# A decoder layer's first stage: new opening for batch 1, block-wise first projection, GpSimd subtractions in four pieces, one name column per slot

## The chip, the cores and the metric

One core of a Trainium2 chip runs the whole kernel as one program. The metric is the device time of one execution in microseconds (us), and the profile is one further execution of the same program. The engines are TensorE (PE; its weight loads are PEld), VectorE (DVE), ScalarE (ACT), GpSimd (POOL) and SyncE (SP, which here only starts DMAs). A line such as L704 is a line of the kernel before.

## The reference, cut to what matters

The input `x` has 8 batches of 512 rows of 512 values. Three residual blocks follow each other; the change touches almost only the first.

```python
x = x + attention(layernorm(x))     # 16 heads of 128, gated, decayed, causal
x = x + cross_attention(layernorm(x), ctx, mask)
x = x + ffn(layernorm(x))           # weights rounded to fp8 after a reordering of columns
# attention, per head: q, k, v = silu(x @ w), scores = (q @ k.T) * decay, out = scores @ v,
#   out = norm_w * out / rms(out), gate = sigmoid(x @ w_gate), y = (gate * out) @ w_out
# ffn: W[:, idx], scaled by the row's largest value, rounded to fp8
```

## The kernel before, in words

**Stages.** `attention` (L171) runs first and takes about three quarters of the time, `finish` (L1057 and on) applies the output projection, the cross attention and the FFN tile by tile. Each has one program for each engine; semaphores written by hand set the order.

**Slots.** The attention stage is a loop of 128 slots (`slots`, L318). Slot n works on head pair p = n // 16, batch b and head j of the pair. In each slot PE does, in this order: the decayed scores of the slot (L788, 12 matmuls), the projections of the next slot's q and k and of this slot's gate (L704, 36 matmuls of 512 columns), whatever extra work the slot has, the product of scores and values (L828, 12) and half of the next values (L713, 24). Every product is done in three passes from a high and a low part of both operands, and DVE makes the low parts: L996 for the scores (`sl`, three instructions, which L828 waits for), L855 for q, k and v, with a cast L853 before it.

**Weights.** Each head pair has four weight blocks (V, QK0, QK1, G) of 128x1024. SP loads them to `raw`, ACT copies the high part (`weights_hi`, L540), POOL subtracts to get the low part (`weights_lo`, L433, one instruction for a block). At the last batch of a head pair (slots 14, 30, 46, and so on, then the slot after) the blocks of the next pair are made; V and QK1 come back to back on POOL.

**x.** Each batch of x has to be normed and turned before it can be used. `stats_of` (DVE, L885, L888) takes mean and variance, `norm` (POOL, L454 to L462) makes the factor and the shift from them, `normed` (ACT, L566) applies them, PE turns (L723, L754 for batch 0) and ACT and DVE split the result (`x_hi` L574, `x_lo` L894). Batches 0 and 1 are prepared in the opening, ahead of slot 0, batches 2 to 7 in the slots 0, 1, 3, 5, 7, 9 (`PREPARED`, L186): SP stores their pieces to DRAM (`store_pieces`, L361) and loads them back (L412) for the batch after next. In each prepared slot PE turns three blocks ahead of L828 and one after.

**Names and rows.** The FFN's reordering indices are counted by `add_name` (DVE, L904): 4 columns of 512 and 11 of 1408, grouped by `SUMMED` (L190) into the slots 11 to 15 as 4, 3, 3, 3 and 2 columns. From slot 18 on, one FFN weight tile is masked (POOL), scaled, rounded (DVE) and turned (PE L746) in every three slots, 26 in all (`FIRST`, `STEP`, L188 and L189).

**Opening.** POOL sets constants and clears `sq_sum` (L498), DVE converts a few of them (L948 to L953), then statistics of batch 0, POOL's `norm(0)`, the norming on ACT, 16 turns on PE, the split, and q and k of slot 0 (L704), the turning of batch 1, and the values of batch 0 in two halves (L713), where the second half waits until DVE has read the first half's bank.

Of the kernel before, what the change touches and what calls it, by code (L numbers as in the profile page):

```python
# [15 lines left out]
P = 128  # L16
# [154 lines left out]
def attention(nc, c, early, at, x, w_src, norm_w, slope, ffn, indices, w_outs, dram):  # L171
# [18 lines left out]
    SUMMED = {NAMED - 5 + i: part for i, part in enumerate(  # L190
        [range(0, KD), range(KD, KD + 3), range(KD + 3, KD + 6), range(KD + 6, KD + 9), range(KD + 9, KD + KF)])}
# [24 lines left out]
    for w in (QK1_W, G_W):  # L216
# [28 lines left out]
    nr, kc = sb("newton", [P, 4, KT]), sb("rstd_consts", [P, 4, KT])  # L245
    rs, nb = sb("rstd", [P, 2, KT]), sb("neg_mean_rstd", [P, 2, KT])
# [18 lines left out]
                for l, start, end in (("hi", at.w_out, at.heads), ("lo", at.shared, at.w_out))]  # L265
# [8 lines left out]
    s_xin = [sem(f"x_in{i}_landed") for i in range(3)]  # L274
    s_raw = [sem(f"raw{i}_landed") for i in range(4)]
    s_nw, s_slope, s_ix = sem("norm_w_landed"), sem("slope_landed"), sem("indices_landed")
    s_wh = [sem(f"w{i}_hi_ready") for i in range(4)]
    s_wl = [sem(f"w{i}_lo_ready") for i in range(4)]
    s_pool, s_kc, s_dist = sem("pool_constants"), sem("rstd_consts_ready"), sem("distance_ready")
# [15 lines left out]
    s_sq, s_acc, s_zero = sem("o_squared"), sem("squares_added"), sem("squares_cleared")  # L295
# [3 lines left out]
    s_mag, s_vs, s_round, s_quant = (sem("rows_magnitude"), sem("rows_scaled"), sem("rows_offset"),  # L299
                                     sem("rows_quantised"))  # L300
# [10 lines left out]
    def x_banks(m):  # L311
        return (*S_BANK, G_BANK if m == 1 else Q_BANK)

    def landed(m):

        return s_xin[X_BUFFER[m]], 16 * X_BUFFER[:m + 1].count(X_BUFFER[m])
# [27 lines left out]
    def sync(sp):  # L344
# [25 lines left out]
        sp.dma_start(slope_b[:, :], slope.to_broadcast([P, NH])).then_inc(s_slope, 16)  # L370
        load_x(0)
# [3 lines left out]
        load_raw(QK1_W, 0)  # L375
        load_x(2)
        load_raw(G_W, 0)
        sp.dma_start(nw[:, :], norm_w).then_inc(s_nw, 16)
        sp.dma_start(uix[:, :], indices[0]).then_inc(s_ix, 16)
        sp.dma_start(dix[:, :], indices[1]).then_inc(s_ix, 16)  # L380
        store_x(0)
        sp.wait_ge(s_turned, KD * 2)
        load_x(3)
        store_x(1)
        for n, v, p, b, j in slots():
            if n % (2 * B) == 0 and p + 1 < NP:
                for w in (V_W, QK0_W, QK1_W, G_W):
                    sp.wait_ge(s_wl[w], p + 1)
                    load_raw(w, p + 1)
            if n == LAST + 1 - 2 * B:  # L390
                for w in range(4):
                    sp.wait_ge(s_wl[w], NP)
# [25 lines left out]
            if n in PREPARED:  # L418
                m = PREPARED[n]
                store_pieces(m)  # L420
                if m != 3 and m + 1 < B:
                    nxt = 4 if m == 2 else m + 1
                    sp.wait_ge(s_turned, KD * m + KD)
                    load_x(nxt)
# [5 lines left out]
    def gpsimd(g):  # L430
        def weights_lo(w, p):
            g.wait_ge(s_wh[w], p + 1)
            g.tensor_tensor(wl[w][:, :], raw[w], wh[w][:, :].bitcast(F32), ALU.subtract).then_inc(s_wl[w], 1)  # L433
# [7 lines left out]
        def norm(m):  # L441
# [3 lines left out]
            if m:  # L445
                g.wait_ge(s_nb, m)
            if m >= 2:
                g.wait_ge(s_nm, KT * (m - 2) + KT)

            def did(k, ins):  # L450
                ins.then_inc(s_nrs, 1)
                g.wait_ge(s_nrs, 8 * m + k + 1)
# [31 lines left out]

        g.memset(c.ident[:, :], 0.0).then_inc(s_pool, 1)
        g.memset(tri[:, :], 1.0).then_inc(s_pool, 1)
        g.iota(dist[:, :].bitcast(I32), [[1, S]], base=0, channel_multiplier=-1).then_inc(s_pool, 1)
        g.wait_ge(s_pool, 3)
        g.affine_select(out=tri[:, :], in_=tri[:, :], compare_op=ALU.is_ge, fill=0.0,
                        base=0, pattern=[[1, S]], channel_multiplier=-1).then_inc(s_pool, 1)  # L490
        g.affine_select(out=c.ident[:, :], in_=c.ident[:, :], compare_op=ALU.not_equal, fill=1.0,
                        base=0, pattern=[[-1, P]], channel_multiplier=1).then_inc(s_pool, 1)
        for k, value in enumerate((LN_EPS, -0.5, 1.5, -1.0)):
            g.memset(kc[:, k, :], value).then_inc(s_kc, 1)
        g.memset(c.ones[:, :], 1.0).then_inc(s_pool, 1)
        g.memset(ones16[:, :], 1.0).then_inc(s_pool, 1)
        g.wait_ge(s_kc, 4)
        g.memset(sq_sum[:, :], 0.0).then_inc(s_zero, 1)  # L498
        norm(0)
        norm(1)  # L500
        weights_lo(V_W, 0)
        norm(2)
        weights_lo(QK1_W, 0)
        weights_lo(G_W, 0)
        for n, v, p, b, j in slots():
# [13 lines left out]
            if n + 1 in PREPARED and PREPARED[n + 1] > 2:  # L519
                norm(PREPARED[n + 1])  # L520
            if n == NAMED - 6:
# [5 lines left out]
            g.wait_ge(s_zero, 1)  # L527
            col_b = slice(b * S, (b + 1) * S)
            if n:
                g.wait_ge(s_acc, n)  # L530
            g.tensor_tensor(sq_sum[:, col_b], sq_sum[:, col_b], sq[:, :], ALU.add).then_inc(s_acc, 1)  # L531
# [5 lines left out]
    def scalar(act):  # L537
# [50 lines left out]
        def sig_values(half):  # L588
# [3 lines left out]
            nc.scalar.activation(sig_v[:, :], V_BANK[:, :], ACT.Sigmoid).then_inc(s_sigv, 1)  # L592

        def scaled(n):
# [4 lines left out]
            nc.scalar.activation(v_mag[:, 0:w], rows[:, 0:w], ACT.Abs, scale=w_s[:, s, 2:3]).then_inc(s_mag, 1)  # L599
# [15 lines left out]
        act.wait_ge(s_slope, 16)  # L615
        act.wait_ge(s_dist, 4)
        decay(0)
        weights_hi(QK0_W, 0)
        normed(0)
        weights_hi(V_W, 0)  # L620
        for k in range(KD):
            x_hi(0, k)
        weights_hi(QK1_W, 0)
# [1045 lines left out]
```

## Time and profile before

| | before |
|---|---|
| median of 3 runs | 2697.77 us (2696.01 to 2700.08) |
| profiled execution, its own time | 2699.37 us |
| span of its profile | 2697.6 us, mean granted clock 0.991 |
| PE busy | 2625.0 us, 97% of the span |
| DVE busy | 2123.9 us, 79% |
| ACT, POOL busy | 1066.4 us, 772.8 us |
| opening, up to the first scores matmul | 43.18 us |

The page gives for each engine its busy time and the costliest groups of instructions. The chain of waits follows the work that ended last back to the start; while it stays on one engine, that engine never waits there. A view of stretches gives the busy time and the granted clock (1.00 is 2.4 GHz, one half of it 1.2 GHz) between two times.

### The profile page before, as it was taken

The numbers are of one execution on the slowest core, as the hardware profiler recorded it, in microseconds if no ns is written. First come the engines' busy times: TensorE is split into PE (matmuls) and PEld (weight loads), VectorE is DVE, ScalarE is ACT, GpSimd is POOL, SyncE is SP. The second block draws the span as 40 slices with busy tenths as digits, with TensorE's granted clock in tenths as the row PEclk, the third lists the DMA queues.
The fourth block names the chain that finished last, engine by engine and source line by source line (L and its number), as shares of the span: only waits on it lengthen the run. The fifth ranks groups of instructions, "written<-read, shape, count | busy, mean of one in ns | idle before, by whom it ended". The sixth has DMA issues, their size and how long they took to land.

```text
span 2697.6 us, 39827 instructions
## 1 busy us (share of the span) xinstructions
PE 2625.0 (97%) x14231; PEld 2173.0 (81%) x14231; DVE 2123.9 (79%) x3806; ACT 1066.4 (40%) x1786; POOL 772.8 (29%) x952
## 2 busy tenths in 40 slices
PE   6999899999999999999999999999999999999995
PEld 6888788888888888888888888888877666666662
DVE  7888977877787778778788867876657888888887
ACT  4433333433343343334344423433324445444553
POOL 3111211221131122112212211211123555555555
PEclk9999999999999999999999999999999999999998
DMA  6553322243233324343334422342265555555532
GB/s 230 180 212 141 128 104 104 102 163 121 102 136 131 122 100 137 105 147 119 126 111 147 157 94 94 118 180 94 94 227 173 148 157 161 151 147 160 162 99 54
DMA packets 182499, 366.67 MB, mean 136 GB/s; under 512 B 79264, under 2 KB 82208, under 8 KB 173600
## 3 DMA queue, kind: packets, MB, share of 16 engines
q1 hardware_dynamic: 116480, 339.74, 36.4%
q10 hardware_dynamic: 63488, 15.74, 3.2%
q0 software_dynamic: 2336, 8.65, 1.0%
q8 instruction: 115, 1.88, 0.3%
q14 instruction: 80, 0.66, 0.1%
HBM read 251.75 MB, written 96.61 MB: 129 GB/s over the span
## 4 chain that ended last, share of the span: by engine, by line
PE 95%; DVE 2%; issue 2%; POOL 0%; DMA 0%; ACT 0%; POOLq 0%; DVEq 0%; SPq 0%; ACTq 0%
PE bank L704 39%; PE bank L713 14%; PE bank L1356 13%; PE bank L828 9%; PE bank L788 9%; PE bank L1397 5%; PE bank L1407 2%; PE bank L1386 1%; PE bank L1377 1%; PE bank L1366 1%; PE bank L723 0%; PE bank L746 0%; DMA finish_xs<-in_pad_mask 0%; DVE finish_rt L1559 0%; DVE finish_u L1457 0%
## 5 line engine op out<-in xcount | busy, mean ns | idle before, releaser
L704 PE MATMUL bank<-attention_xT,attention_w_hi 128*128 128x512 f32 x3072 | 956.5, 392 | 2.7 <-DVE attention_xT L894 2.6
L704 PEld LDWEIGHTS bank<-attention_xT,attention_w_hi 128*128 128x128 f32 x3072 | 568.7, 189 | 114.5 <-issue 3.2
L704 PE MATMUL bank<-attention_xT,attention_w_lo 128*128 128x512 f32 x1536 | 599.6, 390 | 0.0
L531 POOL TENSOR_TENSOR attention_sq_sum<-attention_sq_sum,attention_sq 128x512 f32<-128x512 f32 x128 | 206.6, 1614 | 1228.9 <-ACT attention_sq L676 1228.9
L713 PE MATMUL bank<-attention_w_hi,attention_xT 128*128 128x256 f32 x2048 | 383.6, 288 | 3.7 <-DVE attention_sig_v L851 3.7
L704 PEld LDWEIGHTS bank<-attention_xT,attention_w_lo 128*128 128x128 f32 x1536 | 288.8, 188 | 62.1
L713 PEld LDWEIGHTS bank<-attention_w_hi,attention_xT 128*128 128x128 f32 x2048 | 321.1, 193 | 4.0 <-DVE attention_sig_v L851 4.0
L713 PE MATMUL bank<-attention_w_lo,attention_xT 128*128 128x256 f32 x1024 | 291.1, 284 | 0.0
L1356 PE MATMUL bank<-finish_w_out_hi,finish_og 128*128 128x512 f32 x824 | 284.7, 407 | 0.2
L984 DVE TENSOR_TENSOR attention_sf<-bank,attention_dcy 128x512 f32<-128x512 f32 (+1 forms) x256 | 147.8, 619 | 172.4 <-PE bank L788 172.3
L996 DVE TENSOR_TENSOR attention_sl<-attention_sf,attention_sh 128x384 fp32r<-128x384 f32 (+1 forms) x384 | 242.6, 686 | 0.0
L637 ACT CAST attention_sh<-attention_sf 128x384 fp32r<-128x384 f32 (+1 forms) x384 | 186.0, 548 | 124.2 <-DVE attention_sf L984 123.5
L676 ACT ACTIVATE attention_sq<-bank 128x512 f32<-128x512 f32 x128 | 76.9, 601 | 331.4 <-DVE attention_og L1027 331.4
L1027 DVE SCALAR_TENSOR_TENSOR attention_og<-bank,attention_nw,attention_gate 128x512 f32<-128x512 f32 x128 | 95.8, 748 | 133.8 <-PE bank L828 133.8
L713 PEld LDWEIGHTS bank<-attention_w_lo,attention_xT 128*128 128x128 f32 x1024 | 197.6, 193 | 0.0
L1356 PEld LDWEIGHTS bank<-finish_w_out_hi,finish_og 128*128 128x128 f32 x824 | 154.9, 188 | 39.2 <-issue 2.7
L1204 POOL TENSOR_TENSOR finish_t<-finish_silu,finish_u 128x512 f32<-128x512 f32 (+1 forms) x96 | 133.4, 1391 | 160.0 <-ACT finish_silu L1273 156.7
L828 PE MATMUL bank<-attention_sh,attention_vh 128*128 128x512 f32 (+3 forms) x512 | 162.8, 318 | 14.5 <-issue 14.5
L660 ACT ACTIVATE attention_gate<-bank 128x512 f32<-128x512 f32 x128 | 76.6, 598 | 246.5 <-PE bank L704 246.5
L586 ACT ACTIVATE attention_sig_k<-bank 128x512 f32<-128x512 f32 x128 | 76.6, 599 | 239.5 <-PE bank L704 239.4
L828 PE MATMUL bank<-attention_sh,attention_vl 128*128 128x512 f32 (+3 forms) x512 | 166.7, 326 | 0.0
L828 PE MATMUL bank<-attention_sl,attention_vh 128*128 128x512 f32 (+3 forms) x512 | 166.1, 324 | 0.0
(195 smaller groups left out, 4971.7 us busy)
## 6 DMA issues: line engine op xcount, KB each, us to landing
attention_xT<-normed_turned SPq DMA_DIRECT2D x62, 2048.0 KB, 8.5
gated_heads<-attention_og_out SPq DMA_DIRECT2D x64, 1024.0 KB, 7.3
finish_og<-gated_heads SPq DMA_DIRECT2D x103, 512.0 KB, 3.8
finish_og_last<-gated_heads SPq DMA_DIRECT2D x25, 512.0 KB, 3.8
normed_turned<-attention_shared SPq DMA_DIRECT2D x24, 512.0 KB, 6.6
attention_shared<-in_w_head SPq DMA_DIRECT2D x16, 512.0 KB, 7.1
finish_x<-in_x SPq DMA_DIRECT2D x32, 256.0 KB, 4.0
out<-finish_x SPq DMA_DIRECT2D x32, 256.0 KB, 4.3
```

Source lines behind the costliest of these rows:

```text
L531: g.tensor_tensor(sq_sum[:, col_b], sq_sum[:, col_b], sq[:, :], ALU.add).then_inc(s_acc, 1)
L637: nc.scalar.copy(sh[:, a:e], sf[:, a:e]).then_inc(s_sh, 1)
L704: mm = pe.matmul(dst[:, :], part[a][w][:, k, col:col + P], xT[i][:, b, k, :], start=(k == 0 and s == 0), stop=(k == KD - 1 and s == 2))
L713: mm = pe.matmul(V_BANK[:, t * 2 * P:(t + 1) * 2 * P], xT[i][:, b, k, (2 * j + t) * P:(2 * j + t + 1) * P], part[a][V_W][:, k, :], start=( ...
L788: mm = pe.matmul(dst, (kh, kl)[a][:, t * P:(t + 1) * P], (qh, ql)[e][:, Q0[t]:S], start=(s == 0), stop=(s == 2))
L828: mm = pe.matmul(O_BANK[:, Q0[t]:S], (vh, vl)[a][i][:, t, j * P:(j + 1) * P], (sh, sl)[e][:, OFF[t]:OFF[t + 1]], start=(t == 0 and s == 0) ...
L984: v_.tensor_tensor(sf[:, OFF[k]:OFF[k + 1]], S_BANK[k][:, 0:S - Q0[k]], d[:, 0:S - Q0[k]], ALU.mult).then_inc(s_sf, 1)
L996: v_.tensor_tensor(sl[:, a:e], sf[:, a:e], sh[:, a:e].bitcast(F32), ALU.subtract).then_inc(s_sl, 1)
L1027: v_.scalar_tensor_tensor(out=og[:, :], in0=O_BANK[:, :], scalar=nw[:, 2 * p + j:2 * p + j + 1], in1=gate[:, :], op0=ALU.mult, op1=ALU.mul ...
L1204: g.tensor_tensor(t_[:, a:a + w], sg[k % 2][:, 0:w], u_[k % 2][:, 0:w], ALU.mult).then_inc(s_t, 1)
L1356: mm = pe.matmul(Y_BANK[:, :], og[Q % RING][:, j, a, :], wo[b][:, q * HQ + j, :], start=(q == 0 and j == 0 and s == 0), stop=(q == 3 and j ...
L1397: mm = pe.matmul(dst[:, 0:w], qT[m % 2][:, d, :], wT[:, a // P:(a + w) // P, d, :], start=(d == 0), stop=(d == KD - 1))
```

## The change

- The statistics and the norming of batch 0 go tile by tile: four DMAs for x of batch 0 (the slopes come through ACT's queue), `root_of(0)` on DVE instead of `norm(0)` on POOL, ACT applies it to tiles 0 and 1, DVE to tiles 2 and 3.
- The QK0 block of the first head pair is split in four pieces (ACT high, DVE low), and the first q projection waits for each block of x and weights by itself.
- PE runs 160 matmuls of 128 columns on ones (`keep_warm`) from the start, and 12 more after the turns.
- Batch 1 is prepared in slot 0, all four of its blocks ahead of L828; the others follow in slots 1, 2, 4, 6, 8, 10. The second half of the first values goes to another bank and waits for nothing. `sq_sum` is not cleared; its first use is a copy.
- `weights_lo` is four instructions of 128x256 instead of one of 128x1024.
- Names: one column per slot in slots 12 to 26; the FFN weight tiles start at slot 29 instead of 18.
- SP stores the prepared pieces ahead of its other work of the slot.
- Two waits on ACT's magnitude output are dropped, since a later ACT instruction is waited for anyway. In `finish` the last tile's addition goes from POOL to DVE.

```diff
-    PREPARED = {0: 2, 1: 3, 3: 4, 5: 5, 7: 6, 9: 7}
-    NAMED = 2 * B
+    PREPARED = {0: 1, 1: 2, 2: 3, 4: 4, 6: 5, 8: 6, 10: 7}
+    FOLLOWS = {1: 3, 2: 4, 4: 5, 5: 6, 6: 7}
+    COLUMNS = max(PREPARED) + 1
+    NAMED = COLUMNS + 1 + KD + KF
     FIRST = NAMED + 2
-    SUMMED = {NAMED - 5 + i: part for i, part in enumerate(
+    SUMMED = {COLUMNS + 1 + k: k for k in range(KD + KF)}
...
         def weights_lo(w, p):
-            g.wait_ge(s_wh[w], p + 1)
-            g.tensor_tensor(wl[w][:, :], raw[w], wh[w][:, :].bitcast(F32), ALU.subtract).then_inc(s_wl[w], 1)
+            g.wait_ge(s_wh[w], refreshed(w, p))
+            for k in range(KD):
+                ins = g.tensor_tensor(part[1][w][:, k, :], raw_part(w, k), part[0][w][:, k, :].bitcast(F32), ALU.subtract)
+            ins.then_inc(s_wl[w], 1)
...
-        g.memset(sq_sum[:, :], 0.0).then_inc(s_zero, 1)
-        norm(0)
+        weights_lo(V_W, 0)
+        weights_lo(QK1_W, 0)
         norm(1)
-        weights_lo(V_W, 0)
-        norm(2)
-        weights_lo(QK1_W, 0)
         weights_lo(G_W, 0)
...
+        def keep_warm(times):
+
+            for _ in range(times):
+                pe.matmul(V_BANK[:, 0:P], ones16[:, :], ones16[:, :], start=True, stop=True, skip_group_check=True)
...
+        pe.wait_ge(s_pool, 1)
+        keep_warm(160)
+        pe.wait_ge(s_pool, 4)
+        for t in (0, 2, 1, 3):
...
+        keep_warm(12)
+        for k in range(KD):
+            pe.wait_ge(s_w0h, k + 1)
+            pe.wait_ge(s_w0l, k + 1)
+            pe.wait_ge(s_xl, k + 1)
+            for s, (a, b) in enumerate(PASSES):
+                mm = pe.matmul(Q_BANK[:, :], part[a][QK0_W][:, k, 0:P], xT[0][:, b, k, :],
+                               start=(k == 0 and s == 0), stop=(k == KD - 1 and s == 2))
+        mm.then_inc(s_q, 1)
         head_rows(K_BANK, QK0_W, P, 0).then_inc(s_k, 1)
-        for k in range(KD):
-            turn_x(1, k)
         wait_part(V_W, 0)
         values(0, 0)
-        pe.wait_ge(s_vm, 1)
-        values(1, 0)
+        values(1, 0, v_bank(1))
...
+        def root_of(m):
+
+            st, i = Steps(s_root, 13 * m), m % 2
+            v_.wait_ge(s_st, 2 * KT * m + 2 * KT)
+            rsqrt(v_, st, rs[:, i, :], mv[:, i, :, 1], nr0[:, 0, :], nr0[:, 1, :], 1.0, LN_EPS)
...
+            if m == T - 1:
+                v.wait_ge(s_yo, T)
+                v.tensor_tensor(xr[m % SLOTS][:, :], yo[:, :], xr[m % SLOTS][:, :], ALU.add).then_inc(s_x3, 1)
```

## Rows read from the trace of the kernel before

**Rows 1.** The page: engines (busy us, share, instructions).
```profile
PE 2625.0 (97%) x14231; PEld 2173.0 (81%) x14231; DVE 2123.9 (79%) x3806; ACT 1066.4 (40%) x1786; POOL 772.8 (29%) x952
```

**Rows 2.** Waits of PE, whole span: us in total, times, longest us.
```profile
PE bank L828 <- issue: 14.5, 6, 5.9
...
PE bank L788 <- issue: 3.4, 3, 2.4
```

**Rows 3.** Chain of waits in the opening: start us, us, what.
```profile
10.56 0.21 POOL attention_newton L454
...
21.32 8.02 PE bank L704 x24
...
37.69 5.49 PE bank L713 x24
43.18 2.00 PE bank L788 x12
...
53.41 1.31 PE bank L723 x12
...
57.06 2.88 PE bank L713 x24
```

**Rows 4.** Timeline of the opening: start us, us, engine, line, operation.
```profile
3.28 3.52 POOL L498 MEMSET attention_sq_sum<- 128x4096 f32 x1
...
7.59 2.46 DVE L885 BATCH_NORM_STATS2 attention_stats<-attention_og_out 128x6 f32<-128x512 f32 x4
...
14.07 2.93 ACT L566 ACTIVATE attention_og_out<-attention_og_out,attention_neg_mean_rstd,attention_rstd 128x512 f32<-128x512 f32 x4 [2.75 <-POOL attention_neg_mean_rstd L462]
...
18.69 2.48 DVE L894 TENSOR_TENSOR attention_xT<-bank,attention_xT 128x512 fp32r<-128x512 f32 x4 [2.14 <-ACT attention_xT L574]
```

**Rows 5.** Chain where the finish stage's same root runs on DVE, first step.
```profile
2002.22 0.19 DVE attention_sm L54
```

**Rows 6.** Chain in a later slot: eleven bf16 turns of 128 columns.
```profile
1387.33 0.63 PE bank L746 x11
```

**Rows 7.** Stretches, each from one slot's scores to the next's; clock, DMA share, GB/s last.
```profile
217.76:232.63 14.87, 14.87 (x86) 13.19 (x85) 13.30 (x24) 4.45 (x8) 2.15 (x2) 1.00 0.26 87
262.38:285.18 22.80, 16.88 (x86) 14.72 (x85) 19.86 (x23) 9.80 (x14) 6.60 (x3) 0.85 0.20 80
285.18:301.86 16.68, 15.11 (x84) 12.93 (x84) 16.30 (x24) 5.06 (x9) 4.13 (x2) 1.00 0.34 123
512.54:529.81 17.27, 15.36 (x90) 13.34 (x89) 14.64 (x20) 10.70 (x18) 9.06 (x5) 1.00 0.35 130
994.43:1014.31 19.88, 16.64 (x86) 14.63 (x85) 15.99 (x22) 10.77 (x16) 6.75 (x4) 0.91 0.23 92
1014.31:1029.47 15.16, 15.16 (x89) 13.28 (x89) 13.52 (x22) 6.42 (x13) 5.95 (x4) 1.00 0.34 114
1238.87:1257.67 18.80, 16.89 (x90) 14.83 (x89) 16.17 (x21) 10.82 (x18) 10.40 (x6) 0.91 0.32 120
```

**Rows 8.** Timeline of DVE and POOL around slot 62's wait at 1004.53.
```profile
1002.22 2.41 POOL L433 TENSOR_TENSOR attention_w_lo<-attention_shared,attention_w_hi 128x1024 fp32r<-128x1024 f32 x1 [6.44 <-ACT attention_w_hi L540]
1002.29 2.76 DVE L996 TENSOR_TENSOR attention_sl<-attention_sf,attention_sh 128x384 fp32r<-128x384 f32 x1
1004.60 2.65 POOL L433 TENSOR_TENSOR attention_w_lo<-attention_shared,attention_w_hi 128x1024 fp32r<-128x1024 f32 x1
1004.98 2.69 DVE L996 TENSOR_TENSOR attention_sl<-attention_sf,attention_sh 128x384 fp32r<-128x384 f32 x1
```

**Rows 9.** Timeline of DVE in slots 14 and 15: name columns.
```profile
281.79 5.26 DVE L904 SCALAR_TENSOR_TENSOR attention_shared<-attention_shared,attention_ixf 128x1408 f16<-128x1408 f32 x3
```

**Rows 10.** Timeline of the end of the span: the last tile's addition.
```profile
2693.89 1.26 POOL L1243 TENSOR_TENSOR finish_x<-finish_y,finish_x 128x512 f32<-128x512 f32 x1 [6.54 <-DVE finish_y L1444]
```

**Rows 11.** SP's queue: the first load back of a turned batch.
```profile
70.29 0.33 SPq L412 DMA_DIRECT2D attention_xT<-normed_turned  x1
```

**Rows 12.** The page: DMA issues (line, count, KB each, median us to landing).
```profile
attention_xT<-normed_turned SPq DMA_DIRECT2D x62, 2048.0 KB, 8.5
```

More of the change, by code:

```diff
@@ L311, in x_banks, with before_o, refreshed, v_bank @@
     def x_banks(m):
-        return (*S_BANK, G_BANK if m == 1 else Q_BANK)
+        return (*S_BANK, G_BANK if m < 2 else Q_BANK)
     def landed(m):
-        return s_xin[X_BUFFER[m]], 16 * X_BUFFER[:m + 1].count(X_BUFFER[m])
+        return s_xin[X_BUFFER[m] - 1], 16 * X_BUFFER[:m + 1].count(X_BUFFER[m])
+    def before_o(m):
+        return range(KD if m == 1 else KD - 1)
+    def refreshed(w, p):
+        return p if w == QK0_W else p + 1
+    def v_bank(half):
+        return O_BANK if half == 1 else V_BANK
+    def raw_part(w, k):
+        return raw[w][:, k * 2 * P:(k + 1) * 2 * P]
     def slots():
@@ L591, in sig_values @@
                 act.wait_ge(s_vl, half)
-            nc.scalar.activation(sig_v[:, :], V_BANK[:, :], ACT.Sigmoid).then_inc(s_sigv, 1)
+            nc.scalar.activation(sig_v[:, :], v_bank(half)[:, :], ACT.Sigmoid).then_inc(s_sigv, 1)
         def scaled(n):
@@ L613, in turned @@
             ins.then_inc(s_evac, 1)
-        act.wait_ge(s_slope, 16)
-        act.wait_ge(s_dist, 4)
+        nc.scalar.dma_start(slope_b[:, :], slope.to_broadcast([P, NH])).then_inc(s_slope, 16)
+        act.wait_ge(s_dist, 3)
         decay(0)
-        weights_hi(QK0_W, 0)
-        normed(0)
-        weights_hi(V_W, 0)
+        nc.scalar.activation(warm[:, :], dist[:, 0:1], ACT.Sigmoid)
+        act.wait_ge(s_nb, 1)
+        for t in range(KT // 2):
+            nc.scalar.activation(x_buf[0][:, t, :], x_buf[0][:, t, :], ACT.Identity, bias=nb[:, 0, t:t + 1],
+                                 scale=rs[:, 0, t:t + 1]).then_inc(s_n0, 1)
+        act.wait_ge(s_raw[QK0_W], 16)
+        for k in range(KD):
+            nc.scalar.copy(part[0][QK0_W][:, k, :], raw_part(QK0_W, k)).then_inc(s_w0h, 1)
         for k in range(KD):
             x_hi(0, k)
-        weights_hi(QK1_W, 0)
+        weights_hi(V_W, 0)
         sig_query(0)
         sig_key(0)
+        weights_hi(QK1_W, 0)
+        sig_values(0)
         weights_hi(G_W, 0)
-        for k in range(KD):
-            x_hi(1, k)
-        sig_values(0)
         for n, v, p, b, j in slots():
@@ L668, in scalar @@
             if n in PREPARED:
-                for k in range(3):
+                for k in before_o(PREPARED[n]):
                     x_hi(PREPARED[n], k)
@@ L706, in head_rows, with values @@
             return mm
-        def values(j, i):
+        def values(j, i, bank_=V_BANK):
             for t in (0, 1):
@@ L811, in tensor @@
                 pe.wait_ge(s_sf, 3 * n + 3)
-                for k in range(3):
+                for k in before_o(PREPARED[n]):
+                    if k == KD - 1:
+                        pe.wait_ge(s_gate, n + 1)
                     turn_x(PREPARED[n], k)
@@ L1001, in vector @@
             if n in PREPARED:
-                for k in range(3):
+                for k in before_o(PREPARED[n]):
                     x_lo(PREPARED[n], k)
-            if n + 1 in PREPARED and PREPARED[n + 1] > 2:
-                stats_of(PREPARED[n + 1])
-            if n == NAMED - 6:
+            if n + 1 in PREPARED:
+                all_stats_of(PREPARED[n + 1])
+            if n == COLUMNS:
                 for k in range(KD):
                     v_.wait_ge(s_pst[k], 16 * (B - 2))
-                v_.wait_ge(s_ix, 32)
                 v_.wait_ge(s_col, 1)
```

218 lines of the change are left out of this document (116 added, 102 removed).

## The prediction

> **What bounds the kernel now.** I read the page first. PE is busy for 97% of the span [rows 1], so the time is PE's work plus its waits, plus what it loses at the lower clock. Next I read PE's waits. "Issue" ahead of L828 (scores by values) comes six times with 14.5 us together, ahead of L788 three times with 3.4 us [rows 2]. The third view is the chain, cut at the opening: slot 0's scores start at 43.18 us [rows 3], and nearly all of PE's idle time before them is there. The fourth is a cut of the attention stage into slots. A plain slot takes 14.87 us, one that also turns an FFN weight tile 15.16, and then PE is busy for all of it at clock 1.00 [rows 7]. DVE is busy for 13.30 us of the plain one, so it is second and near. The stretches at the change of a head pair are longer than that, and only there is something to be won besides the opening. The last view is the timeline inside such a stretch [rows 8]. It shows what the wait is made of; the reader should look for DVE instructions that take five times their length.
>
> **Part 1, the opening.** In order of what ends last. First DVE: the clearing of `sq_sum` on POOL lasts 3.52 us from 3.28 [rows 4] and the statistics start only at 7.59; afterwards no such instruction is there and the tiles of x arrive one by one. The load of x is issued at about 0.8 instead of 1.3, so I let the last tile's statistics (2.46/4 = 0.62, plus an aggregate) end at about 8.0, against 10.5, when POOL's chain starts now [rows 3]. The root then is 13 dependent instructions plus one for the shift. The finish stage has one such step at 0.19 us with the next a little behind it [rows 5], so 14 x 0.21 = 2.9 us, where POOL's chain takes from 10.56 to 14.07, 3.5 us [rows 3, 4]. Norming can start at 10.9 instead of 14.07. It is two tiles on each of two engines, 2 x 0.73 = 1.5 us instead of 2.93 [rows 4]. So x is normed at 12.4.
>
> PE by then must be through its 160 matmuls. Eleven bf16 turns of 128 columns take 0.63 us at full clock [rows 6], 0.057 each, and I take twice that, 0.114, at 1.2 GHz. Now PE starts the first projection at 21.32 and gets its full clock only during it; the 24 value matmuls from 37.69, after an idle stretch, take 5.49 us where the same 24 take 2.88 later [rows 3]. So five us or so pass at half speed after a start. From 1.05 to 6 that is 43 of the 160, the other 117 take 6.7 us, end 12.7. The turns of batch 0 (16, of which 12 take 1.31 us at full clock [rows 3], so 1.75) end at 14.5. ACT's first copy is done at 15.2, DVE's four subtractions take 2.48 us [rows 4] and end at 17.8; the first projection follows block by block and ends 0.7 us behind, 18.5. The k projection is a third of 36 matmuls of which 24 now take 8.02 us partly at low clock [rows 3]; at full clock a third of the 36 is 2.75, so 21.3. Two halves of values at 2.88 each follow without the wait between them: slot 0 starts at 27.1. Beside them lie DVE's queries, the statistics of batch 1 and the keys, by my count until 26.1; those are queued one behind the other, so this cover is 1 us thick, and if it is gone each us costs one. POOL makes V's low part by about 21, just before PE wants it (21.3); what is queued behind it (QK1, `norm(1)`, G) is wanted by PE at 29, by ACT at 30 and by PE at 34.
>
> Gain 43.18 - 27.1 = 16.1 us. Against it stands that batch 1 now is turned in slot 0, a slot more that turns (1.8 us, as above). Its fourth block waits for the gate's sigmoid, and the values of batch 1, 2.88 us later in the same slot, wait for all of it split: 0.3 us. And batch 2 is prepared one slot later, in slot 1, behind it SP has a load of 1 MB and then the load back of batch 2, which waits for the last piece to be stored. Now that load goes at 70.29 [rows 11], 10 us into slot 1; after, its last piece is split about 18 us into slot 1 (DVE has statistics in front of it), so it goes 22 to 23 us after slot 1's start, lands 8.5 us later [rows 12], at 31, and is wanted at 16.8 + 13.9 = 30.7. So 0 to 2 us, I take 0.4. The opening is worth 16.1 - 1.8 - 0.7 = **13.6 us**, bounds 10 and 16.
>
> **Part 2, the subtractions in four pieces.** Slot 62 shows the mechanism. POOL subtracts from 1002.22 for 2.41 us, a DVE subtraction of 384 columns that starts at 1002.29 takes 2.76, ending with POOL's plus 0.4. The second pair does the same, POOL from 1004.60 for 2.65, DVE from 1004.98 for 2.69 [rows 8]. So a DVE instruction that reads two SBUF operands stands still until POOL's current instruction is through, and it gets in between two of POOL's. PE meanwhile waits for exactly these `sl`. The Trainium skill, "SBUF — State Buffer", section "Who interferes with whom", says that such a pair is locked for the whole instruction, and that DVE's instructions with two SBUF inputs are among those that meet it. By that rule the block is as long as one piece; the trace agrees, 2.76 and 2.69 us against 2.41.
>
> A piece of 256 columns: 1024 cost 2.41 [rows 8] and 512 cost 1.26 [rows 10], so 2.25 us per 1000 columns and 0.1 fixed, 0.7 us. The two blocked `sl` then take about 1.05 each instead of 2.7: 3.3 us sooner in every stretch in which two whole blocks fall on them. The excess of the stretches shown is 22.80 - 14.87 = 7.93, 16.68 - 14.87 = 1.81, 17.27 - 15.16 = 2.11, 19.88 - 14.87 = 5.01 and 18.80 - 15.16 = 3.64, in all 20.5 us [rows 7]. It is more than the waits, because the clock falls after the long ones (0.85, 0.91, 0.91 in these rows). They hold 14.5 us of the waits; those not touched (2.4 at the stage's end) left out, 1 us more of [rows 2] lies at two other changes of pair. I take 21.5 us as the stock. The waits themselves there are 1.9 (twice) and 3.24, all below 3.3, so they go to zero or near. What comes late next are the queries and keys: four DVE instructions behind `sl` that now each may meet a piece (4 x 0.7), and PE wants them 4.8 us after it could start L828. By my count they come 0.5 us ahead of that.
>
> **Part 3, names.** Slot 14 holds three columns of 1408 (5.26 us [rows 9]) and two more slots before it do too, so DVE enters it late. Afterwards slot 14 and 15 have one of 512 each and slots 16 to 26 one of 1408, 1.75 us on a DVE that is busy 13.3 of 14.87 with 4 columns of 512 in it [rows 7]; without those and with one long one it is less. So this part clears slots 14 and 15 together with part 2. The row tasks move 11 slots later; 26 tasks remain 26 tasks, in slots of the same slack. Parts 2 and 3 leave 1.2 us of the 21.5: **20.3 us**, bounds 13 and 22.
>
> **Part 4, the rest.** The last tile's addition on DVE costs about 0.7 (a two-input subtraction of 512 there, a quarter of 2.48 [rows 4]) instead of 1.26 [rows 10]: **0.6 us**. The dropped waits, the copy in place of an addition and the order of SP's stores cost and give nothing on the path; ACT and POOL have over half their time free [rows 1].
>
> **The sum.** 13.6 + 20.3 + 0.6 = 34.5 us. The profiled execution took 2699.4, so a run like it takes 2664.9; the median is 1.6 lower, 2663.3. I say 2664.
>
> **Rivals.**
> *Pieces that don't let go.* The four pieces have no wait between them, so POOL may run from one into the next and hold DVE for 2.4 us as now. The two pieces seen with DVE between them [rows 8] had a semaphore wait ahead of the second, though ACT had long met it, so they speak against this but don't exclude it. The excess of slot 14 and 15 would then fall from 9.7 to about the mean of the other pairs (2.11, 5.01, 3.64 and two small ones, 2.5): 7.2 instead of 20.3, total 21.4, time 2676.5. The Trainium skill, "GPSIMD Engine Reference", section "Instruction dispatch", says that consecutive GpSimd instructions are no barrier between its cores, each goes on with the next as it ends its share. By that rule the gap might vanish; no run here shows it yet. Chance 0.1.
> *PE not warm.* The dummy matmuls don't raise the clock, or PE's own queue is slower than 0.057 us each. At 0.114 throughout they end at 1.05 + 18.2 = 19.3, 6.6 us after my 12.7, and the turns and projections at 1.2 GHz may cost 2 to 4 us more. Opening 3 to 7, total 24 to 28, time about 2672. For it: nothing shows a matmul on ones. Against it: in all other stretches PE at work gets 1.00. Chance 0.1.
> *Slower.* Every piece may block another DVE instruction, 12 pieces in the two slots of a change of pair at 0.8 us each, 9.6 us of DVE time where now it is 3 blocks of 2.7, on an engine that already is busy for 16 us or more in these stretches [rows 7]. If PE then waits for queries and keys for x us at each of 7 changes, the kernel is slower by more than 0.2% from 7x = 21.5 + 14.2 + 5.4, x = 5.9 us. It would need DVE to lose 6 us more than it loses now; the alternation gives POOL part of its time beside DVE's PSUM readers. Price at x = 6.5: 2709. Chance 0.03.
> *Within 0.2%.* Rival one and two together, and cover lost in slot 0: 0.03.
>
> **How the numbers follow.** My forecast, with its bounds, has 0.74; its own range is 2659 to 2672. Rivals one and two reach to 2678. The range that should hold 8 in 10 is 2656 to 2679. A measurement of this kernel tells 0.2%, 5.4 us, from no change. Faster by more 0.94, within it 0.03, slower 0.03.
>
> **What the profile will show.** Right: PE's first real turn at about 12.7 with clock 1.00, slot 0's scores at 26 to 28; a slot 14 of under 16 us; DVE `sl` ones of 1.0 to 1.2 us beside pieces of 0.7; no long "issue" ahead of L828 between 270 and 1520. Wrong, by part: scores of slot 0 after 31 (opening); `sl` still at 2.7 (rival one); 1.2 GHz between 12 and 20 us (rival two); a new wait ahead of L788 for queries and keys at the changes of pair (the slower case, or its small form). A wait at the end of slot 2 for the load back would be the 0.4 us term at its other end.

## The result

| | before | changed |
|---|---|---|
| median | 2698.65 us (4 runs) | 2663.85 us (2663.56 to 2664.57, 4 runs) |
| ratio of the changed kernel to the one before | | 0.9875 (95%: 0.9862 to 0.9888) |
| profiled execution | 2699.37 us | 2663.93 us |
| span, mean granted clock | 2697.6 us, 0.991 | 2662.2 us, 0.995 |

The change takes 34.8 us off the median and 35.4 off the span. The prediction said 34.5 and 2664 us. Two places carry it, the opening and the changes of head pair. The first gave 0.9 us less than forecast and the second 2.1 us more, so it is luck that the sum is so near.

The page's first row of the changed kernel, to be read beside [rows 1], and three of its waits of PE over the whole span, beside [rows 2] (us in total, times, longest):

```profile
PE 2623.2 (99%) x14403; PEld 2174.1 (82%) x14403; DVE 2104.0 (79%) x3822; ACT 1068.8 (40%) x1792; POOL 790.2 (30%) x1034
```
```profile
PE bank L831 <- issue: 2.4, 1, 2.4
...
PE bank L748 <- DMA attention_xT<-normed_turned: 0.7, 1, 0.7
PE bank L739 <- DVE attention_shared L953: 0.5, 1, 0.5
```

PE has 172 matmuls more and yet 2 us less of busy time, at 99% of the span. The six waits ahead of the product of scores and values (14.5 us in [rows 2]) are gone. Ahead of the scores (now L831) only the one of 2.4 us near the end of the stage is left, which was there before. Between 250 and 1930 us PE now waits for nobody.

The chain of waits of the changed kernel in the opening, beside [rows 3] (start us, us, what):

```profile
0.83 4.48 DMA attention_slope<-in_slope
...
5.51 0.61 DVE attention_stats L927
...
8.73 0.18 DVE attention_newton_first L54
...
11.39 1.52 ACT attention_og_out L643 x2
...
15.47 2.98 PE bank L804 x12
...
41.15 3.11 PE bank L748 x24
44.26 1.85 PE bank L831 x12
```

And its stretches from one slot's scores to the next's (slots 0, 1 and 2, then 14 and 46, two changes of head pair), beside [rows 7]. After the length come the busy times of PE, PEld, DVE, ACT and POOL, the clock, the DMA share and GB/s:

```profile
27.00:44.26 17.26, 16.99 (x103) 15.14 (x102) 16.83 (x33) 8.57 (x15) 5.95 (x12) 1.00 0.32 120
44.26:60.90 16.64, 16.64 (x102) 14.91 (x101) 15.25 (x31) 8.51 (x15) 3.27 (x11) 1.00 0.58 205
60.90:79.15 18.25, 17.04 (x101) 14.95 (x101) 14.92 (x27) 10.07 (x18) 4.63 (x10) 1.00 0.86 314
```
```profile
249.69:264.56 14.87, 14.87 (x85) 13.20 (x85) 13.19 (x19) 8.40 (x13) 7.17 (x9) 1.00 0.33 122
728.41:743.29 14.88, 14.88 (x86) 13.20 (x85) 12.04 (x17) 9.16 (x13) 7.30 (x9) 1.00 0.33 122
```

Slot 14 took 22.80 us before. The reader should compare the last row, slot 46, with the 19.88 us of slot 62 in [rows 7]; in both a row task is in its rounding step. GpSimd is busy for longer (7.30 us against 6.75), DVE for less (12.04 against 15.99, and most of that difference was standing still), and PE is busy for all of the slot.

The balance comes from the starts of three slots' scores in the chains. Slot 0 starts at 27.00 instead of 43.18. Slot 11 starts at 217.76 before [rows 7]; in the changed kernel it is

```profile
205.07 1.85 PE bank L831 x12
```

so 12.7 us of the gain are there by slot 11. Slot 126 is the first line in the kernel before and the second in the changed one:

```profile
1966.61 1.85 PE bank L788 x12
```
```profile
1931.47 1.85 PE bank L831 x12
```

35.1 us by then, so 22.4 us between slots 11 and 126, and 0.3 us for all of the rest. From slot 126 to the end the executions of kernels with one and the same code there differ by more than that (730.9 us in the changed kernel, 729.3 in the one without dummy matmuls), so the last row of the table tells nothing either way.

| place | predicted | measured |
|---|---|---|
| opening with slots 0 to 10 | 13.6 | 12.7 |
| changes of head pair | 20.3 | 22.4 |
| the end | 0.6 | 0.3 |

### The profile page after: what moved, and what is told of

It reads as the page before. It is cut to its first block, busy times and chain, and to the rows that moved or that the text cites. A ratio compares the mean times of both kernels' runs of the same rounds, so it can differ in the third digit from the quotient of the medians.

```text
span 2662.2 us, 40188 instructions
## 1 busy us (share of the span) xinstructions
PE 2623.2 (99%) x14403; PEld 2174.1 (82%) x14403; DVE 2104.0 (79%) x3822; ACT 1068.8 (40%) x1792; POOL 790.2 (30%) x1034
## 4 chain that ended last, share of the span: by engine, by line
PE 94%; DVE 3%; DMA 1%; issue 1%; ACT 0%; POOL 0%; SPq 0%; DVEq 0%; POOLq 0%; ACTq 0%
PE bank L739 39%; PE bank L748 14%; PE bank L1415 13%; PE bank L831 9%; PE bank L873 9%; PE bank L1456 5%; PE bank L1466 3%; PE bank L1445 1%; PE bank L1436 1%; PE bank L1425 1%; DMA attention_xT<-normed_turned 0%; PE bank L781 0%; DMA finish_xs<-in_pad_mask 0%; DVE attention_stats L927 0%; PE bank L758 0%
## 5 line engine op out<-in xcount | busy, mean ns | idle before, releaser
L553 POOL TENSOR_TENSOR attention_sq_sum<-attention_sq_sum,attention_sq 128x512 f32<-128x512 f32 x120 | 191.8, 1599 | 1095.4 <-ACT attention_sq L702 1095.2
L1055 DVE TENSOR_TENSOR attention_sl<-attention_sf,attention_sh 128x384 fp32r<-128x384 f32 (+1 forms) x384 | 226.8, 646 | 0.0
L831 PE MATMUL bank<-attention_ql,attention_kh 128*128 128x512 f32 (+3 forms) x512 | 165.7, 324 | 0.0
```

The lines of the kernel that those rows point to most:

```text
L831: mm = pe.matmul(dst, (kh, kl)[a][:, t * P:(t + 1) * P], (qh, ql)[e][:, Q0[t]:S], start=(s == 0), stop=(s == 2))
L1055: v_.tensor_tensor(sl[:, a:e], sf[:, a:e], sh[:, a:e].bitcast(F32), ALU.subtract).then_inc(s_sl, 1)
```

## Experiments on the subtractions and the names

The first four take the changed kernel and undo something. The theory is that a DVE instruction with two SBUF operands stands still until GpSimd's current instruction ends, so that the length of one piece sets what PE waits. Its rival is that the names made the wait.

**One piece again.** In `weights_lo`:

```diff
-            for k in range(KD):
-                ins = g.tensor_tensor(part[1][w][:, k, :], raw_part(w, k), part[0][w][:, k, :].bitcast(F32), ALU.subtract)
-            ins.then_inc(s_wl[w], 1)
+            g.tensor_tensor(wl[w][:, :], raw[w], wh[w][:, :].bitcast(F32), ALU.subtract).then_inc(s_wl[w], 1)
```

> The changed kernel with one GpSimd subtraction of 1024 columns for each weight block again, all else kept. Lock theory: DVE's score subtractions stand still 2.7 us each again at the changes of head pair (slots 14, 30, 46, 62, 78, 94), PE waits ahead of the product of scores and values there, 1.5 to 5 us of excess in most of these slots, 12 to 15 us in all: about 2677 us. Rival (the names were what cost, the pieces nothing): 0 to 2 us more than the changed kernel, 2664 to 2666 us. The opening stays as it is, slot 0's scores at 27 us.

Measured: 2677.35 us, 13.5 more than the changed kernel, as the theory said. The stretches of slots 46, 62 and 94:

```profile
729.45:749.10 19.65, 16.41 (x85) 14.24 (x85) 15.77 (x22) 10.76 (x16) 6.52 (x4) 0.91 0.24 94
973.66:990.93 17.27, 15.36 (x90) 13.34 (x89) 14.64 (x20) 10.69 (x18) 9.06 (x5) 1.00 0.33 127
1455.55:1475.46 19.91, 16.67 (x86) 14.56 (x85) 16.02 (x22) 10.77 (x16) 6.77 (x4) 0.91 0.23 93
```

4.8, 2.1 and 5.0 us of excess over 14.87, 15.16 and 14.87. Slot 14 has none: with one short name column even the whole blocks fit there. The large excess sits where a row task is in its rounding step (46 and 94, and 62 in the kernel before). ACT's scaling a slot earlier makes the values' sigmoid late and DVE's subtractions with it: the sigmoid starts 5.0 us into slots 46 and 94, 3.9 us into slot 62 and 2.6 us into slots 30 and 78. In those last two only one of the three subtractions meets a block (2.75 us; another takes its free 0.55), and there is no excess.

**Two pieces of 512.**

```diff
+            for k in range(2):
+                cols = slice(k * RAW // 2, (k + 1) * RAW // 2)
+                ins = g.tensor_tensor(wl[w][:, cols], raw[w][:, cols], wh[w][:, cols].bitcast(F32), ALU.subtract)
+            ins.then_inc(s_wl[w], 1)
```

> The changed kernel with two pieces of 512 columns instead of four of 256. Lock theory, by the length of one piece (1.26 us): two blocked score subtractions cost 3.2 us, against 5.4 with one piece and 2.1 with four; only the two changes where a_whole has 5 us (slots 46 and 94) keep an excess, about 1.3 us each: 2666 to 2667 us. Rival (what counts is the total time of GpSimd, not the piece): the same as a_whole, 2677.

Measured: 2665.88 us, 2.0 more than with four pieces and 11.5 less than with one. The three DVE subtractions of slot 46 (each fence one line of the timeline: start, us) with one piece, with two and with four:

```profile
736.70 5.99 DVE L1053 TENSOR_TENSOR attention_sl<-attention_sf,attention_sh 128x512 fp32r<-128x512 f32 x3
```
```profile
735.11 3.82 DVE L1056 TENSOR_TENSOR attention_sl<-attention_sf,attention_sh 128x512 fp32r<-128x512 f32 x3
```
```profile
734.52 2.71 DVE L1055 TENSOR_TENSOR attention_sl<-attention_sf,attention_sh 128x512 fp32r<-128x512 f32 x3
```

Not blocked they take 1.62. One by one the last two, of 384 columns, take 2.77 and 2.69 us, 1.65 each and 1.10 each, where 0.55 is their free length. So two of the three wait for one piece each, and the time falls with the length of the piece while GpSimd's work stays the same or grows. This settles the mechanism. The Trainium skill's rule on the shared pair, in "SBUF — State Buffer", section "Who interferes with whom" (held for a whole instruction), agrees with all three rows. The Trainium skill's rule that consecutive GpSimd instructions are no barrier between its cores ("GPSIMD Engine Reference", section "Instruction dispatch") had been a reason for a rival in which four pieces hold DVE like one; the 2.71 us rule that out here.

The block is not one of instructions with two SBUF operands alone. Behind the subtractions DVE casts the queries, one SBUF operand in and one out, beside the pieces (changed kernel, slot 46):

```profile
737.88 0.94 DVE L898 CAST attention_qh<-attention_sig_q 128x512 fp32r<-128x512 f32 x1
```

The same cast takes 0.43 us elsewhere. And GpSimd pays too: a piece takes 0.74 us by itself and 1.05 to 1.19 where DVE's subtractions meet it.

**Names in five slots again.** `NAMED` is `COLUMNS + 6` and the columns go as 4, 3, 3, 3, 2 into slots 12 to 16, with `for k in SUMMED.get(n, ()): add_name(k)` on DVE.

> The changed kernel with the name columns in five slots again (12 to 16: 4, 3, 3, 3, 2 columns), four pieces kept. Theory (names and pieces both load DVE at the first change of pair): DVE enters slot 14 late by the long columns of slot 13, an excess of 2 to 5 us in slots 14 to 16 together and none at the other changes: about 2668 us. Rival (the block by GpSimd alone made the wait of slot 14, DVE has slack for the columns): no excess, 2664 us.

Measured: 2671.83 us, 8.0 more. The mechanism is as expected, the size not: three slots in a row with three long columns, 5.1 us each, are more than DVE's slack also with short pieces. Slots 14 to 16 hold 7.3 us of it. The chain of waits at that place shows DVE as the engine that is behind, name columns first:

```profile
266.26 1.68 DVE attention_shared L964
267.99 0.04 issue
268.04 1.70 DVE attention_shared L964
...
278.37 1.63 issue
280.00 2.09 PE bank L874 x12
...
295.11 1.36 issue
296.46 2.10 PE bank L874 x12
```

**Both undone.** The two edits together.

> The changed kernel with both undone, one subtraction of 1024 columns and names in five slots. Additive: a_whole plus what a_grouped adds, about 2681 us. Not additive (the two meet in slot 14, as in the kernel before, where that slot and the next had 9.7 us of excess): 22 us of excess, 2686 us.

Measured: 2692.63 us, 28.8 more, where the parts add up to 21.5. They are not additive, and this is even more than what the kernel before loses there (22.4). In the profiled execution slots 14 to 16 have 9.9 us of excess, 2.5 more than with the names alone, since the names and the blocks meet in slot 14. Later slots have 16 us, where the blocks alone cost 13 and the names alone 1: the row tasks now start at slot 19, so that their rounding step falls on slots 30 and 78 and their masking on 46 and 94. This execution is one of the shorter ones (2689.43 us); what the others lose beyond it no profile shows.

**Each part alone on the kernel before.** First the four pieces, as above with `cols = slice(k * 2 * P, (k + 1) * 2 * P)`.

> The kernel before with its GpSimd weight subtractions in four pieces, nothing else. Lock theory: no excess at slots 30, 46, 62, 78 and 94, where the kernel before has about 12 us, and less in slots 14 and 15, where the columns of names remain (3 to 6 us of the 9.7): gain 16 to 19 us, 2680 us. Rival (the gain of the pieces needs the new order of names or the new opening): under 10 us, above 2688.

Measured: 2683.38 us (2680.44 to 2685.84), ratio 0.9948 (0.9931 to 0.9965), 14.9 us less than the kernel before in the same runs. A little short of the expected gain; the profile has no excess at slots 30 to 94, but 7 us in slots 14 and 15 from the names.

Then the names, one per slot from slot 11, row tasks from slot 28.

> The kernel before with one name column per slot (slots 11 to 25, row tasks from slot 28), nothing else. Theory: slots 14 and 15 lose their 9.7 us, since a_whole shows none there; at the other changes of pair the excess goes by which step of the row task falls on it (the rounding step 5 us, masking 2, scaling 0.5), now 30: 5, 46: 2, 62: 0.5, 78: 5, 94: 2, so 14.5 us instead of 12.4: gain about 7.5 us, 2690 us. Rival (GpSimd's block alone holds slot 14): gain 2 us or less.

Measured: 2694.95 us, ratio 0.9990 (0.9980 to 0.9999), so 3.3 us, less than half of what was expected. The profiled execution is the fastest of ten, 2690.31 us, and in it the model holds: the wait of slot 14 is gone and slot 30, which now has the rounding step, shows

```profile
501.30:521.18 19.88, 16.64 (x85) 14.63 (x85) 15.99 (x22) 10.76 (x16) 6.75 (x4) 0.91 0.23 91
```

which is slot 62 of [rows 7] to the digit, but for the DMA rate. In the other nine executions 4 to 6 us more are lost, at a granted clock of 0.989 to 0.990 instead of 0.993. Where, no profile shows; that stays open.

The names alone give little, since they move the costly step onto two other changes of pair. The pieces alone give most of it. Together they give 22.4.

## Experiments on the opening

**Without the dummy matmuls.** Both calls of `keep_warm` are taken out of the changed kernel.

> The changed kernel without the 172 dummy matmuls of the opening. Clock theory: batch 0's turns start at 12.4 us as now but at 1.2 GHz (3.6 us instead of 1.9), the first projection runs at half speed too, the full clock comes 5 us or so after it starts; slot 0's scores at 31 to 32 us instead of 27.0, time 2668 to 2669 us. Rival (PE is covered by DVE and ACT there, or the dummies' own length of 11 us costs what they give): within 1 us of the changed kernel.

Measured: 2664.83 us, 1.0 more than the changed kernel, with ranges that overlap (2663.51 to 2665.82 against 2663.56 to 2664.57). That is the rival's time. Of the theory the first half was right and the second wrong. PE in the timeline of this kernel:

```profile
12.51 3.50 PE L793 MATMUL bank<-ident,attention_og_out 128*128 128x128 f32 x16 [12.51 <-ACT attention_og_out L643]
17.01 0.70 PE L802 MATMUL bank<-attention_xT,attention_w_hi 128*128 128x512 f32 x2 [1.00 <-DVE attention_xT L951]
17.55 0.40 PE L802 MATMUL bank<-attention_xT,attention_w_lo 128*128 128x512 f32 x1
```

The turns run at 1.2 GHz, 3.50 us instead of 1.94, but the projection runs at full clock from its start (0.40 us for a matmul that took 0.63 in the kernel before). So the 172 dummies hide 1.6 us of turning: slot 0's scores start at 27.00 with them and at 28.55 without. How much of it arrives in the time the two ranges leave open.

Why the full clock came before the first projection here and during it in the kernel before is not shown. It is tempting to name the pause between turns and projection (2.65 us there, 1.00 here), but the last turn of this run already takes 0.27 us and the first ones 0.42, so the clock rose at 15.7 us, ahead of the pause; in the kernel before all 16 take 0.42 or more, 3.65 us together. And it rose at different times in executions in which PE did the same until then. Two kernels further up, the kernel before with only the four pieces and with only the names moved, have the opening of the kernel before. Their chains show the first two projections as (pieces, then names)

```profile
21.33 7.12 PE bank L707 x24
```
```profile
21.31 8.61 PE bank L703 x24
```

to be read beside the 8.02 us in [rows 3]. With the pieces, with the names and in the kernel before the matmuls shorten from 0.63 to 0.39 us at 24.3, 27.5 and 26.3 us, and slot 0's scores start at 41.43, 42.65 and 43.18 us. So almost 2 us of the old opening belong to one execution and not to its code, and the 12.7 us measured for the opening are no surer than that.

**Without the clearing.** In the kernel before, the clearing of `sq_sum` is taken out and its first use is a copy.

> The kernel before without clearing sq_sum on GpSimd in the opening (its first use copies, as in the changed kernel), nothing else. Theory (the statistics wait for the load of x, which lands at about 7.5 us, 6.2 us after its issue at 1.27): DVE's casts end 3 us earlier, and nothing later moves, 0 to 0.3 us of gain, 2698 us. Rival (the prediction's reading, the clearing holds DVE): statistics from about 4.5 us, slot 0's scores 3 us earlier.

Measured: 2699.49 us, ratio 1.0006 (0.9996 to 1.0015), no gain. The timeline of DVE:

```profile
3.80 0.43 DVE L953 TENSOR_SCALAR attention_dist<-attention_dist 128x512 f32<-128x512 f32 x1
7.19 2.47 DVE L885 BATCH_NORM_STATS2 attention_stats<-attention_og_out 128x6 f32<-128x512 f32 x4 [2.97 <-DMA attention_og_out<-in_x]
```

DVE is free at 4.2 instead of 7.7 us and then waits for x until 7.19. The rival, which was the prediction's own reading, is refuted: the statistics start 0.4 us sooner and not 3, and what releases them is the DMA of x.

The clearing did hold DVE. In the kernel before, this cast beside it

```profile
3.06 3.81 DVE L948 CAST ident_bf<-ident 128x128 bf16<-128x128 f32 x1 [3.06 <-POOL ident L491]
```

took 3.81 us, and 0.36 without it. But x was not there before 7.2 us. And the 0.4 us are lost again, the other way round: DVE now subtracts a weight block while GpSimd begins the root, and of GpSimd's chain the first step

```profile
10.23 1.02 POOL attention_newton L454
```

took 0.21 us in [rows 3]. Norming starts at 14.82 instead of 14.07. Slot 0's scores come 1.0 us sooner in the profiled execution all the same, at 42.16, since PE got its full clock at 25.1 instead of 26.3 us.

In the changed kernel four DMAs of a quarter each, and statistics that follow them one by one, bring the end of the statistics from 10.5 to 8.7 us.

**The other bank alone.** In the kernel before, the second half of the first values goes to `O_BANK` and PE's wait for `s_vm` goes.

> The kernel before with the second half of the first values in the other bank, so that PE doesn't wait for DVE's reading of the first half; nothing else. Theory: PE goes on at 33.9 instead of 37.7 and doesn't fall to 1.2 GHz, slot 0's scores at 36.8 to 37.5 instead of 43.2, gain 5 to 6 us if DVE keeps up. Rival (DVE is what ends last there: statistics of batch 2, the split of batch 1 and the values before the scores): slot 0 is longer by what its scores come earlier, gain under 2 us.

Measured: 2693.45 us, ratio 0.9984 (0.9975 to 0.9994), 4.2 us for the 5 to 6 of the theory. Slot 0's scores start at 37.22, inside the expected 36.8 to 37.5, and then a wait appears that was hidden (waits of PE):

```profile
PE bank L704 <- POOL attention_w_lo L433: 1.9, 1, 1.9
```

QK1's low part is queued behind `norm(2)` on GpSimd. The changed kernel puts both weight blocks ahead of the norm; its V and QK1 parts are ready at 21.0 and 25.6 us, and PE takes them at 21.2 and 28.9.

So the 16.2 us up to slot 0's scores come apart like this, from the timelines of PE before and after: 8.2 us up to the end of the k projection (29.2 against 21.0), 1.9 us for the turns of batch 1 that moved into slot 0, and the remaining 6.1 us for the wait between the halves of the values with the half-speed matmuls behind it.

**The statistics of batch 3 later.** In the changed kernel, DVE's order in slot 1:

```diff
-            if n + 1 in PREPARED:
+            if n + 1 in PREPARED and n != 1:
                 all_stats_of(PREPARED[n + 1])
...
+            if n == 1:
+                all_stats_of(PREPARED[n + 1])
```

> The changed kernel with batch 3's statistics behind, not ahead of, slot 1's gated output and the split of batch 2's last block on DVE. Theory: the last piece of batch 2 is split and stored 3 us sooner, the load back lands before PE asks at the end of slot 2, and the wait ahead of slot 2's projections goes too: slots 1 and 2 take 33.4 us together instead of 34.9, 1.5 us of gain, 2662.3 us. Rival (the load back ends late by the traffic of the other loads, not by its start): gain under 0.6 us.

Measured: 2663.44 us, 0.4 less with overlapping ranges, and the profiled executions are alike (2663.93 us each), so the rival's size holds. The chain of this kernel, with that of the changed kernel behind it:

```profile
59.95 5.10 DMA normed_turned<-attention_shared
...
65.20 10.25 DMA attention_xT<-normed_turned
75.45 0.25 issue
75.70 3.10 PE bank L748 x24
```
```profile
63.14 3.69 DMA normed_turned<-attention_shared
...
66.98 8.81 DMA attention_xT<-normed_turned
```

The last piece is stored 3.2 us sooner, its store takes 1.4 us longer, the load back starts 1.8 us sooner and takes 1.4 us longer, and it lands 0.3 us earlier, of which 0.2 is that slot 0 began sooner. The four stores, the load of batch 4 and the load back share the DMA engines, which in the changed kernel are busy for 0.86 of slot 2. That a transfer which starts sooner is the longer one for this reason is the likely reading; no run changes the traffic alone. The wait ahead of slot 2's projections (0.5 us in the changed kernel) did go, and the wait for the load back took it over.

## Experiments on the rest of the span

**The output weights in pieces.** The same cure for the one wait that is left, in `w_out_lo`:

```diff
+            for h in range(q * CH, (q + 1) * CH):
+                for a in (0, D // 2):
+                    ins = g.tensor_tensor(early.wo[1][:, h, a:a + D // 2], raw_out[:, h, a:a + D // 2],
+                                          early.wo[0][:, h, a:a + D // 2].bitcast(F32), ALU.subtract)
+            ins.then_inc(s_wlo, 1)
```

> The changed kernel, with GpSimd's subtractions for the output weights (w_out_lo, 1024 columns each) in four pieces too. Lock theory: the wait of 2.4 us ahead of the last slot's scores and the low clock behind it (together 4 us) go: 3 to 4 us less than the changed kernel, 2660 to 2661 us. Rival (the last slots wait for ScalarE's copies or for the DMA of the mask, so the time comes back ahead of the output projection): 0 to 1 us less.

Measured: 2662.13 us, 1.7 less. The wait of 2.4 us ahead of the last scores is gone, and a new one of 1.2 us stands a little later in the same slot, ahead of the product of scores and values: the last slot has 12 projection matmuls instead of 36 to cover it. About half of the expected gain arrives.

**All of it together.** The two edits above, 150 dummies, the slopes multiplied behind the first tile's statistics, and in `finish` DVE's `masks()` moved from ahead of `root_of_squares` to behind the first additions.

> The changed kernel with all that the runs point to: a_order, a_wout, the slopes multiplied behind the first tile's statistics (they land at 5.3 us and hold DVE), 150 dummy matmuls instead of 160, and in the finish stage the mask prepared behind the root of the squares instead of ahead of it, since its DMA of 7 us stands on the chain to the first residual addition (PE waits 4.6 us there). Theory: 1.5 + 1.7 + 0.3 + 4 = 7.5 us less than the changed kernel, 2656 us. Rival (the DMA's wait only moves behind the first additions, PE then waits at the first cross attention): 3.5 us less, 2660 us.

Measured: 2660.07 us (2659.23 to 2661.07), ratio 0.9858 (0.9841 to 0.9874) to the kernel before, 3.8 less than the changed kernel. The wait for DVE's first addition was 4.6 us there. Now two of PE's waits stand at the same place:

```profile
PE bank L1421 <- DMA finish_og<-gated_heads: 2.3, 1, 2.3
...
PE bank L1421 <- DVE finish_x L1531: 1.1, 1, 1.1
```

The mask's DMA is off the chain, and the load of the gated heads, 11.3 us on that chain, took its place. It is the fastest of the kernels here, and it got the rival's time, not the theory's.

## Why the prediction was right

**The bound.** PE at 97%, with the idle time of the attention stage in the opening and at the changes of pair: right, and after the change PE waits for nobody between 250 and 1930 us. The prediction's words hold for that stage alone. Of the 73 us in which PE was idle in the kernel before, 28 are waits of the finish stage, with this as the first:

```profile
PE bank L1407 <- DMA finish_tT<-down_named: 11.2, 2, 6.9
```

They are 29 us in the changed kernel. The prediction doesn't name them; that cost it nothing here, as the change hardly touches them, but the last experiment above takes part of its gain there.

**Part 1, the opening.** Right up to slot 0, with errors that cancelled. Slot 0's scores were put at 27.1 and came at 27.00; the dummies were to end at 12.7 and ended at 12.06; the first projection was to end at 18.5 and ended at 18.5. But a reading behind it was wrong: the clearing on GpSimd was named as what held the statistics, and the run without it shows the DMA of x. The statistics ended at 8.7 us for 8.0 forecast. A step the prediction missed is that the slopes, now on ACT's queue, land 4.5 us after their issue instead of 2.7, and DVE stands behind them until 5.33.

The terms that were mis-sized are those set against it, 0.7 us together. The load back at the end of slot 2 was given as "0 to 2 us, I take 0.4". The wait itself was 0.7, and 0.5 came ahead of slot 2's projections for batch 2's last block, which the prediction did not see. Slot 2 takes 18.25 us where the later slots that turn take 16.61 (94.02 to 110.63 in the chain), so 1.6 us in all. Its place and its bounds were right. Slot 0's term, 0.3 for batch 1's split, was 0.3 in the waits, but the slot takes 17.26 us, 0.65 over 16.61. Against that stand 0.6 us that the old slots 0 to 10 lost too. Together they make 12.7 of 13.6, and the 0.9 missing is less than what the start of the old slot 0 varies by (41.43 to 43.18).

**Part 2, the pieces.** Right, also in size. "About 1.05 each" for the blocked subtractions means 2.8 us for the three, measured 2.71. A piece was put at 0.7; it takes 0.74 by itself, and eight take 7.09 us with DVE between them. The queries and keys did get later (their casts take 0.94 instead of 0.43 and their subtractions 1.11 instead of 0.69), and came in time. The 1.2 us set aside for what remains were not needed, the excess is zero at every change; the stock itself was 22.4 rather than 21.5, so that the gain lies just above the upper bound given for it, 22. "A DVE instruction that reads two SBUF operands" was too narrow, as the casts show; it cost nothing, because the sum had let each of the four instructions meet a piece.

**Part 3, the names.** Right as a condition: with them grouped, 8.0 us come back. Its reach is smaller than the prediction's words make it. What it does alone is 3.3 us, since slot 14's wait needs both, and since the shift of the row tasks changes which change of pair is the dear one. That they moved to "slots of the same slack" holds only with the short pieces.

**Part 4.** 0.6 was forecast, 0.3 is left over, which is within what this stretch varies. DVE's last addition takes 0.69 us as said, where GpSimd's took 1.26; PE's wait for the first addition of the finish stage grew from 3.8 to 4.6 us, for the mask's DMA took 7.3 instead of 6.5 us (6.4 in the run with the output weights in pieces, so this too varies).

**The rivals.** "Pieces that don't let go" is refuted by the 2.71 us. "PE not warm" did not occur: the dummies ended at 12.06 us. Of its price one part was tested by taking the dummies out: turns at 1.2 GHz cost 1.6 us up to slot 0, for the 2 to 4 given for turns and projections. The 6.6 us for dummies that are slow throughout and make PE late were not tested. The slower case needed 6 us of new waiting at each change; there is none.

## What to carry to other kernels

Where DVE and GpSimd both work on SBUF, cut GpSimd's work by what the waiting engine can bear, not by what is best for GpSimd: here four pieces cost it 0.8 us more in a slot (7.30 us in slot 46 against 6.52 with one piece) and gave back 13.5 us in the kernel. A dear step that recurs every third slot and one that recurs every sixteenth should be laid out together, since moving one moves which of the meetings is costly. And a wait at the end of a chain of DMAs need not get shorter when the last one starts sooner: here 1.8 us of head start left 0.3.

## What was not expected of the hardware

- The clock. In executions of three kernels with the same opening, in which the first projection starts at 21.3 us, the full clock came at 24.3, 26.3 and 27.5 us. In the kernel without dummies it came 3.2 us after the first turn, while PE was turning; in the kernel before, 3.65 us of the same turns ended without it, and it came 4.9 us into the projection.
- DVE and GpSimd hold each other in both directions, and not only with two SBUF operands: a cast of 0.36 us took 3.81 beside GpSimd's clearing, and a GpSimd step of 0.21 us took 1.02 beside DVE's subtraction.
- A small DMA on ACT's queue beside four larger ones on SP's landed 4.5 us after its issue; alone at the head of SP's queue it took 2.7.
- The same store and the same load, started 3.2 and 1.8 us sooner, each took 1.4 us longer.
